# A fused attention and routed-FFN block on one core: rows of maxima unhindered on SyncE's queue, and the narrow value products of twelve steps in blocks of three

## The reference, cut to what matters

```python
# B, S, D = 2, 1024, 512; 32 query heads of 16, ONE key head and ONE value head; 8 experts of rank 16, the best 2 used
x = hidden_states                                   # (2, 1024, 512), float32
qkv = layernorm(x) @ Wqkv                           # 512 -> 512 queries + 16 keys + 16 values
scores = einsum('bqhd,bkd->bhqk', q, k) * 16 ** -0.5
scores = where(pos_k <= pos_q, scores + slope[h] * (pos_k - pos_q), -1e30)
probs = softmax(scores)
x = x + einsum('bhqk,bkd->bqhd', probs, v).reshape(B, S, 512) @ Wo
y = layernorm(x)
logits = y @ W_gate.T
route = top-2 of softmax(logits), made to sum to 1, as a weight per expert
x = x + y @ W_base.T + b_base + einsum('ner,eor->no', (y @ A.T) * route, B)
```

## Time and profile before

| | before |
|---|---|
| median of 3 runs | 735.76 us |
| profiled execution, its own time | 734.06 us |
| its span | 732.3 us |
| PE busy | 678.6 us (93%), 4304 matmuls |
| DVE busy | 558.6 us (76%) |
| ACT busy | 358.3 us (49%) |
| POOL busy | 216.4 us (30%) |
| TensorE's granted clock, mean | 0.979 |
| DMA moved | 56.32 MB, 77 GB/s |

### The profile page before, as it was taken

One profiled execution on the slowest core, in us unless ns is written; L12 is line 12 of the kernel. 1 busy time (PEld: TensorE's weight loads), 2 busy tenths in 40 slices (PEclk: granted clock), 3 DMA queues, 4 the chain that ended last, 5 costly groups with the idle time before them and its releaser, 6 DMA issues.

```text
span 732.3 us, 13261 instructions
## 1 busy us (share of the span) xinstructions
PE 678.6 (93%) x4304; PEld 309.6 (42%) x4304; DVE 558.6 (76%) x1801; ACT 358.3 (49%) x511; POOL 216.4 (30%) x366
## 2 busy tenths in 40 slices
PE   4979379999999999999999999599999999999997
PEld 2435135354444444444443443234333345555553
DVE  6798468978897888988889999398894166666665
ACT  2313246565656666566666666276676711111111
POOL 0036302223415143351423421224233132222221
PEclk9999789999999999999999999799999999999999
DMA  8567880001222081244108009790000069900001
GB/s 247 119 138 130 151 112 27 32 16 40 87 84 83 17 126 29 100 60 83 56 10 140 26 17 135 119 113 34 17 34 17 16 135 169 185 29 29 30 29 57
DMA packets 42951, 56.32 MB, mean 77 GB/s; under 512 B 6648, under 2 KB 26232, under 8 KB 42752
## 3 DMA queue, kind: packets, MB, share of 16 engines
q1 hardware_dynamic: 40296, 51.27, 35.8%
q10 hardware_dynamic: 2592, 4.26, 1.7%
HBM read 35.72 MB, written 19.79 MB: 76 GB/s over the span
## 4 chain that ended last, share of the span: by engine, by line
PE 71%; DVE 12%; DMA 8%; SPq 4%; ACT 3%; issue 2%; POOL 1%; DVEq 0%; POOLq 0%; ACTq 0%
PE psum L748 16%; PE psum L700 14%; PE psum L730 10%; PE psum L776 8%; PE psum L798 7%; PE psum L646 6%; PE psum L727 4%; DVE psum L1111 4%; DVE negm L1116 3%; DMA q_dram<-arena 3%; DMA m_dram<-m_part 3%; PE psum L793 2%; SPq L470 2%; ACT work L933 2%; PE psum L808 2%
## 5 line engine op out<-in xcount | busy, mean ns | idle before, releaser
L933 ACT ACTIVATE work<-psum 128x1024 f32<-128x1024 f32 (+1 forms) x320 | 288.9, 943 | 150.7 <-PE psum L730 130.8
L1111 DVE CUSTOM_DVE_ANT_0 psum<-psum,future 128x384 f32<-128x384 f32 (+3 forms) x512 | 239.6, 514 | 44.4 <-PE psum L700 39.4
L700 PE MATMUL psum<-k_op,arena 106*128 106x512 bf16 (+3 forms) x768 | 215.5, 331 | 10.4 <-DVE negm L1111 5.6
L1116 DVE TENSOR_REDUCE negm<-psum 128x1 f32<-128x512 f32 x256 | 167.1, 687 | 13.5 <-PE psum L700 10.3
L730 PE MATMUL psum<-arena,k_op 109*128 109x512 bf16 (+3 forms) x640 | 158.9, 318 | 13.6 <-DMA arena<-m_dram 11.5
L1288 POOL TENSOR_SCALAR_AFFINE_SELECT work<-work 128x512 f32<-128x512 f32 x128 | 81.4, 638 | 303.7 <-ACT work L933 303.7
L748 PE MATMUL psum<-work,v_op 128*32 128x512 f32 (+3 forms) x1536 | 164.5, 501 | 2.6 <-POOL work L1288 2.2
L700 PEld LDWEIGHTS psum<-k_op,arena 106*128 106x128 bf16 x768 | 70.4, 98 | 150.6 <-DVE negm L1111 60.7
L727 PE MATMUL psum<-arena,k_op 116*128 116x128 bf16 x512 | 84.7, 221 | 10.1 <-DMA arena<-m_dram 8.8
L646 PE MATMUL psum<-arena,wqkv_sb 128*128 128x256 f32 (+3 forms) x240 | 90.1, 471 | 1.3 <-ACT arena L855 1.3
L730 PEld LDWEIGHTS psum<-arena,k_op 109*128 109x128 bf16 x640 | 59.7, 98 | 54.9 <-ACT work L933 13.5
(11 more groups left out here) (86 smaller groups left out, 443.9 us busy)
## 6 DMA issues: line engine op xcount, KB each, us to landing
arena<-q_dram SPq DMA_DIRECT2D x96, 128.0 KB, 5.1
o_dram<-o_sb SPq DMA_DIRECT2D x32, 256.0 KB
q_dram<-arena SPq DMA_DIRECT2D x16, 384.0 KB, 4.8
arena<-o_dram SPq DMA_DIRECT2D x32, 128.0 KB, 10.8
arena<-rcp_dram SPq DMA_DIRECT2D x32, 128.0 KB, 11.4
out<-wqkv_sb ACTq DMA_DIRECT2D x16, 256.0 KB, 2.0
x_sb<-in_x SPq DMA_DIRECT2D x3, 1024.0 KB, 7.7
work<-in_x SPq DMA_DIRECT2D x3, 1024.0 KB, 18.1
```

What stands on the lines that cost most here:

```text
L700: last = nc.tensor.matmul(bank[:, a * width:(a + 1) * width], q_op[0:ROW_MAX, bass.ds(col, P)], k_op[0:ROW_MAX, b, k0:k0 + width], start=T ...
L933: nc.scalar.activation(probs[:, n % 4, heads * hp:heads * (hp + 1), 0:w], src, ACT.Exp).then_inc(exp_done, 1)
L1111: last = nc.vector.tensor_tensor_reduce(keys, keys, future[:, CH - width:CH], -1.0, 3e38, ALU.add, ALU.min, negm[:, late, 0, j * QT + t:j ...
L1116: nc.vector.tensor_reduce(dst, psum[:, bank, 0:len(js) * width].rearrange("p (a k) -> p a k", a=len(js)), AX_X, ALU.max, negate=True).then ...
```

## The change

On SP: query items 6 and 7 are no longer stored before row of maxima 1; `SPLIT_AT` now gives them to steps 1 and 2 on POOL and SP, and they are loaded after these steps, with the constants of head groups 2 and 3. Items 14 and 15 are loaded ahead of step 11 and not behind it. The two blocks of 16 head loads are cut in eight groups of four (`HEADS_AT`), one behind each row of maxima of steps 11 to 14.

For pairs 3 to 14 (`wide`), whose work fills steps 4 to 15: the ring has six tiles, the fifth and sixth in `x_sb`; the value products of tiles 1, 2, 3 are done in one block at tile 5, those of 9, 10, 11 in one block in the next step at tile 1, and each other one two tiles behind its scores, as before. exp waits for whatever tile had the same place of the ring before (`PROBS_BEFORE`).

```diff
@@ constants and pe_order
+WIDE_FROM = 3
+PV_TRIPLES = {2: (0,), 5: (1, 2, 3), 6: (4,), 7: (5,), 8: (6,), 9: (7,), 10: (8,)}
+
+def wide(m):
+    return WIDE_FROM <= m < NK - 1
+
+def values_at(k, n):
+    out = []
+    late = k - 2
+    if 0 <= late < NK and n < LAG:
+        if not wide(late):
+            out.append((late, (n - LAG + NTI,)))
+        elif n == LAG - 1:
+            out.append((late, (9, 10, 11)))
+    m = k - 1
+    if 0 <= m < NK and n >= LAG:
+        if not wide(m):
+            out.append((m, (n - LAG,)))
+        elif n in PV_TRIPLES:
+            out.append((m, PV_TRIPLES[n]))
+    return out
...
-        m, v = (k - 1, n - LAG) if n >= LAG else (k - 2, n - LAG + NTI)
-        if 0 <= m < NK:
-            work.append((UH * (CH - TILES[v][2]) + PV_FIXED, ("values", m, v)))
+        for m, some in values_at(k, n):
+            work.append((sum(UH * (CH - TILES[v][2]) for v in some) + PV_FIXED, ("values", m, some)))
...
+def probs_slot(m, n):
+    return n % (6 if wide(m) else 4)
+
+def probs_before():
+    out, last = {}, {}
+    for m in range(NK):
+        for n in range(NTI):
+            out[m, n] = last.get(probs_slot(m, n))
+            last[probs_slot(m, n)] = NTI * m + n
+    return out
...
-SPLIT_AT = {3: 8, 4: 9, 5: 10, 6: 11, 7: 12, 8: 13, 9: 14, 10: 15}
+SPLIT_AT = {1: 6, 2: 7, 3: 8, 4: 9, 5: 10, 6: 11, 7: 12, 8: 13, 9: 14, 10: 15}
+HEADS_AT = {11: (0, 0), 12: (0, 2), 13: (1, 0), 14: (1, 2)}
@@ tiles
+        def probs_of(m, n):
+            r = probs_slot(m, n)
+            return ring[:, r] if r < 4 else x_sb[:, r - 4]
@@ block.sync
-            def load_heads(c):
+            def load_heads(c, some=range(UH)):
...
-                for j in range(UH):
+                for j in some:
@@ block.sync, step
                     max_rows(2 * k, i)
+                if k in HEADS_AT:
+                    c, j = HEADS_AT[k]
+                    load_heads(c, (j,))
                 if 1 <= k <= NK:
                     store_unit(2 * k - 2, i)
                 if k < NK:
                     max_rows(2 * k + 1, i)
+                if k in HEADS_AT:
+                    load_heads(c, (j + 1,))
@@ block.sync, the list
-            store_queries(6)
-            store_queries(7)
             max_rows(1)
+            step(1)
             load_constants(2)
+            load_queries(6)
+            step(2)
             load_constants(3)
-            load_queries(6)
             load_queries(7)
-            step(1)
-            step(2)
             step(3)
...
             step(10)
             store_rcps(0)
-            step(11)
             load_queries(14)
             load_queries(15)
-            load_heads(0)
-            step(12)
-            load_heads(1)
-            for k in range(13, NK + 2):
+            for k in range(11, NK + 2):
                 step(k)
@@ block.tensor, values_product and step
-                                            probs[:, n % 4, j, 0:CH - off], start=(t == 0), stop=(t == last_tile))
+                                            probs_of(m, n)[:, j, 0:CH - off], start=(t == 0), stop=(t == last_tile))
...
-                        values_product(m, n, None)
+                        for v in n:
+                            values_product(m, v, None)
@@ block.scalar, exps
-                if NTI * m + n >= 4:
-                    act.wait_ge(pv_done, at_loop(NTI * m + n - 3, i, 2 * NTI))
+                if PROBS_BEFORE[m, n] is not None:
+                    act.wait_ge(pv_done, PROBS_BEFORE[m, n] + 1)
@@ block.gpsimd, before the steps
-            for n in range(3, 8):
+            for n in range(3, 6):
                 split_queries(n)
             split_max(1, None)
```

More of the change, by code:

```diff
@@ L225 @@
 SLOT_AT, USE_AT = places()
-SPLIT_AT = {3: 8, 4: 9, 5: 10, 6: 11, 7: 12, 8: 13, 9: 14, 10: 15}
+def probs_slot(m, n):
[7 more added lines that the diff above has]
+    return out
+PROBS_BEFORE = probs_before()
+SPLIT_AT = {1: 6, 2: 7, 3: 8, 4: 9, 5: 10, 6: 11, 7: 12, 8: 13, 9: 14, 10: 15}
+HEADS_AT = {11: (0, 0), 12: (0, 2), 13: (1, 0), 14: (1, 2)}
 def uses_behind(k):
@@ L278, in build @@
         work = sb("work", [P, 4 * UH * CH])
-        probs = work[:, :].rearrange("p (r j q) -> p r j q", r=4, j=UH)
+        ring = work[:, :].rearrange("p (r j q) -> p r j q", r=4, j=UH)
         xnT = arena[:, 0:2 * KC * CH].rearrange("p (r k q) -> p r k q", r=2, k=KC)
@@ L932, in exps @@
                         src = psum[:, b0:b0 + 2].rearrange("p b q -> p (b q)")[:, 0:UH * w].rearrange("p (j q) -> p j q", j=UH)
-                    nc.scalar.activation(probs[:, n % 4, heads * hp:heads * (hp + 1), 0:w], src, ACT.Exp).then_inc(exp_done, 1)
+                    nc.scalar.activation(probs_of(m, n)[:, heads * hp:heads * (hp + 1), 0:w], src, ACT.Exp).then_inc(exp_done, 1)
                     for u in behind.get((n, hp), ()):
@@ L1286, in zero_future @@
                     plain_next()
-                    d = probs[:, n % 4, :, 0:P]
+                    d = probs_of(m, n)[:, :, 0:P]
                     nc.gpsimd.affine_select(out=d, in_=d, compare_op=ALU.is_ge, fill=0.0, base=0,
```

## The result

The changed kernel takes 728.27 us, the median of 4 runs (724.57 to 729.89), against 736.36 (734.52 to 738.42) for the kernel before: a ratio of 0.988, 95% interval 0.984 to 0.993. It is faster beyond the noise, but by 8 us (under 2%) where 19 were forecast, and lies above the range of the forecast (709.5 to 725.0). The profiled execution took 729.89 us, its span is 728.1. Lines have moved by some fifty: slots are L752, scores L779 and L782, value products L800, turns L733, reductions L1164 and L1169, exp L986, the row's store L549 and load L556.

What follows compares the result with a forecast made beforehand. PE's list was taken as the bound (71% of the chain), DVE close behind in steps 10 to 15. 734.06 - 4.6 - 11.1 - 3.0 = 715.4, plus 1.7 for the median: 717 us, own range 712 to 722, wider range 709.5 to 725.

Steps and rivals of the forecast that it cites:

- Part 1, row 1: Start of step 1: the row's store lands 4.2 us after issue at 84.12; PE goes on 4.6 us sooner.
- Part 2, the heads: Step 13: with head loads in groups of four, PE's wait and the low clock go, 11.1 us saved.
- (c): Step 13: the heads don't fit between the rows, half of 11.1 is kept back, 722.5 us; chance 0.06.
- (d): Steps 12 to 15: groups of four make rows late, each costing 11.1 us, 761 us in all; chance 0.03.
- Part 3, the blocks: Steps 4 to 15: blocks of three value products gain 0.25 us a step, 3.0 over twelve.
- Seams: Value products in blocks: four seams of 0.21 us saved, 0.84 a step, 10.1 over twelve steps.
- The two new waits for ACT: Before score pieces (1, 0) and (5, 0): PE waits 0.52 and 0.56 us for exp, 1.08 a step.
- The third term: Existing waits of 0.8 us a step, mostly for DVE: 0.5 goes away while PE waits for ACT.
- worst: Steps with blocks: new waits count in full, no old ones go, last exp adds its own; 0.45 a step lost, 5.4.
- Rival (b): Steps with blocks: ACT takes more than seams give, 0.45 a step lost, 725.5 us; chance 0.20.
- Rival (a): Steps with blocks: the whole seam saving comes through, 710 us; chance 0.15.
- Ring, copies, rows 2 and 3, items 14 and 15: Larger ring, later bank 7 copies, SP's moves around rows 2 and 3, earlier items 14 and 15: all cost nothing.

Runs made afterwards that it cites:

- e1: The changed kernel with no blocks of three and value products as before, only SP's and POOL's new order; 721.76 us, ratio 0.982.
- e4: The changed kernel with unmasked reductions looking at half of their columns from step 10 on; 723.04 us in a single execution.
- e8: The changed kernel with the fourth slot in a row ahead of each block moved behind it in steps 10 to 15; 723.28 us (one).
- e9: The changed kernel with the first slot of three or four ahead of a block moved ahead of the score piece before them; 723.10 us.
- e2: The changed kernel with the ring of six tiles kept but each value product done by itself; 720.86 us, ratio 0.981.
- e10: e9, blocks in all twelve steps, with row of maxima 1 moved ahead of the load of query item 4; 713.55 us, ratio 0.968.
- e5: The changed kernel without blocks, with unmasked reductions looking at half of their columns from step 10 on; 719.36 us in a single execution.
- e6: The changed kernel with the slots ahead of a block dealt half ahead of it and half behind; 729.62 us, ratio 0.991.
- e11: The changed kernel with only the block of products 1 to 3, products 9 to 11 one by one; 721.65 us, ratio 0.979.
- e13: The changed kernel with only the block of products 9 to 11, products 1 to 3 one by one; 724.67 us, ratio 0.985.
- e3: The changed kernel with blocks only for pairs 3 to 8, the work of steps 4 to 9; 719.43 us, ratio 0.977 left out as unstated; interval 0.975 to 0.982.
- e7: e3 with row of maxima 1 moved ahead of the load of query item 4 on SP; 710.40 us, ratio 0.964.

## Why the prediction was wrong, point by point

**Part 1, row 1: right in kind, 4.6 forecast, 1.5 to 2.2 got.** The row's store was issued 0.4 later than said. The landing was mis-sized: from the store to the row's load 5.7 us, not 4.2. "A 12 KB store can hardly pass them" and "adds little" both held: it landed 0.17 us after the last of the six loads, and 0.16 to 0.20 after it in all eleven kernels with this order. The wrong step was the reading of the earlier trace rows: 4.2 is the median of the six, each from its own issue, and the last one needs more (5.1 before, 5.5 now). Another 0.55 passed between the landing and the issue of the row's load. The wait was 8.12, where 6.5 to 7.5 was said. And a microsecond of wait saved in front of a low clock is not one saved: measured from the turn ahead of it, PE went on 3.65 us sooner (19.22 after the turn against 22.87) and the step became 1.45 shorter; up to 1.7 of the difference is half of the second stretch of 3.4 us at half speed. In e1, without that stretch, 2.9 sooner made 2.1. The views of before showed a clock that stayed low to 97.7; I did not ask whether it would stay low as long.

**Part 2, the heads: right.** 11.1 forecast, 38.74 - 27.61 = 11.13 in e1, 38.74 - 29.18 and the 1.57 of the blocks in the changed kernel. Rivals (c) and (d) have nothing for them: the rows of steps 12 to 14 land in 1.4 to 2.5 us.

**Part 3, the blocks: wrong, and this is what put the time above the range.** Seams held: 0.84 a step forecast, 0.89 measured in step 14 (2.90 to 2.01). The two new waits for ACT held one by one: 0.52 and 0.56 forecast, 0.47 and 0.53 in step 14. Their sum did not count in full, since two waits ahead of other score pieces (0.18 and 0.21) went away: gaps ahead of score pieces grew by 0.77, not 1.08. The third term failed: "While PE waits for ACT, DVE works off its three banks, so most of that 0.8 goes away: I say 0.5." In steps 10 to 15 the waits for banks grew, from 0.63 to 2.32, so the term was +1.7 where -0.5 was said. Nor was there so much to take away: of the 0.8 of waiting in step 14 of the kernel before, 0.39 stood ahead of score pieces and 0.44 ahead of slots, so it was not "mostly for DVE". The sentence is true of the moment of the wait and blind to what the list holds next: with three products moved into one block the slots that stood between them stand in a row, four for three banks, and then nothing feeds DVE for 1.4 us. DVE is busy 25.5 of 27.61 us, so what it idles there may come back as PE's wait, but 3.7 us less for it took only 0.38 off the 1.57. In steps 5 to 9 only three slots are in a row ahead of a block, and the term was +0.02. There the total came out nearly as said, -0.34 for -0.25 (30.52, 30.6 forecast), but by luck: seams gave 1.05, not 0.84, score pieces lost 0.68, not 1.08, and the 0.5 of waits for banks did not come back at all.

Even the "worst" of +0.45 a step was too low, because it bounded the waits for ACT and let the old ones stand; a new wait for DVE was in no term. Rival (b) had the right direction, and the sign given for it (steps above 27.6) came, but its 0.45 a step is 5.4 us for twelve steps; measured were 9.1 lost in six of them and 2.1 gained in the others, 7.0 in all, 6.5 by the medians (728.27 - 721.76). Its words were about ACT's wait starving DVE; the larger part is the waits for banks, 1.69 against 0.77, and they go with the place of the slots around the block: e4 keeps the first of them with a lighter DVE, and in e8 and e9 moving one slot gives 0.97 and 1.15 back. How the rest comes about, which stays with three in a row, no run shows by itself. Rival (a) has nothing for it. The Trainium skill (TensorEngine Tiling (Array Packing), PSUM Bottleneck) says that tiling speeds up TensorE but not the emptying of PSUM, which may then limit; here the banks of other work were what PE waited for (2.32 us of gaps ahead of slots in step 14), not the products' own.

**Ring, copies, rows 2 and 3, items 14 and 15:** at nothing, as said (e2; steps 2 and 3 unchanged). Sum with the measured terms: 734.06 - 0.54 - 11.13 - 2.08 + 9.11 + 0.47 = 729.89, the profiled execution.

What stays open: why the clock falls a second time in one execution and not in another of the same kernel (e10's runs lie 5.4 us apart), and why in step 8 the early block alone takes 0.4 of score waits away and the late one adds to them. The second fall, at 102 to 108 us, is in the traces of the changed kernel and of e4, e5, e6, e8, e11 and e13 and not in those of e1, e2, e3 and e9, so with blocks and without them; e8 and e10 have such a stretch near 400 us too. That makes it likely that the blocks are not its cause, but no run isolates it.

## What to carry to other kernels

When work is drawn together in an in-order list, look at what it leaves behind: count how many producers for the same buffers now stand in a row, and compare it with the number of buffers; with one more than buffers, PE waited 0.6 us for DVE here, and DVE then idled as long while the block ran. A count that is not passed is no promise, though: with three in a row e8 and e9 still lost 0.6 and 0.4 us a step, and slots put in a row behind the block (e6) cost too. So decide step by step: here the early block alone gave 0.8 us in one kind of step and cost 0.7 in another. A sum that comes out right in one kind of step may do so with wrong terms. And a small transfer that something waits for goes ahead of the bulk transfers, not merely ahead of some: cutting the queue from eight items to six ahead of the row gave 2 us, putting it ahead of the loads of items 4 and 5 gave 9 more.

## What the hardware showed

- A 12 KB store behind six loads of 128 KB on one queue landed 0.16 to 0.20 us after the last of them in eleven kernels, 4.9 to 5.6 us after its own issue; the median of the stores of rows was 1.4. The loads, issued 0.35 to 0.5 us apart, need longer one after another: 3.0 us for the first and 5.5 for the sixth in the changed kernel.
- The low clock at the start of step 1 ended at 97.5 in the changed kernel, 96.5 in e1 and 97.7 before, though PE went on at 91.9, 91.9 and 94.6; where PE did not wait for the row (e7) it ended at 87.8. It can fall for 3.4 us under a PE that is busy throughout.
- A step's length repeats to 0.01 us from kernel to kernel when its list and the clock are the same (27.60 or 27.61 in seven kernels); an effect of 0.1 us a step is seen in one execution, though the whole kernel's runs lie 5 us apart.
